# A decoder layer's cross attention: unnormalised exponentials are turned and weighed, and the reciprocal sums, spread over rows by transposes, are applied to the result

## The reference

```python
qh = split_heads(q @ Wq.T + bq); kh = split_heads(k @ Wk.T + bk); vh = split_heads(v @ Wv.T + bv)
scores = einsum('bhqd,bhkd->bhqk', qh, kh) * scale
scores = where(mask == 0, -1e9, scores)
probs = softmax(scores, axis=-1)
out = einsum('bhqk,bhkd->bhqd', probs, vh)
return concat_heads(out) @ Wo.T + bo
```

## Time and profile before

| | |
|---|---|
| median of 3 runs | 1627.44 us (1622.18 to 1630.48) |
| the profiled execution | 1640.67 us |
| its span | 1638.9 us |
| PE busy over the span | 1342.1 us (82%) |
| ACT busy | 893.5 us (55%) |
| DVE busy | 845.1 us (52%) |
| POOL busy | 805.4 us (49%) |
| cross attention | about 764 to 1084 us of the span |

### The profile page before, as it was taken

How to read it: one execution, slowest core, us unless ns; L and a number is a source line. 1 busy time by engine, 2 the same in 40 slices (tenths; PEclk the granted TensorE clock), 3 DMA queues, 4 the chain that set the end, 5 groups by cost and what they waited for, 6 DMA issues and landing times. The chain is left out here.

```text
span 1638.9 us, 31788 instructions
## 1 busy us (share of the span) xinstructions
PE 1342.1 (82%) x10439; PEld 1127.5 (69%) x10439; DVE 845.1 (52%) x1783; ACT 893.5 (55%) x2002; POOL 805.4 (49%) x847
## 2 busy tenths in 40 slices
PE   4999999999999999997877877732699999988300
PEld 4788888888878788885655655522588888887300
DVE  3344444544444444452666576649354454456337
ACT  4677676777767677774255555510355455455101
POOL 2344343444434344454466767601556756667464
PEclk9999999999999999998899999965799999999655
DMA  3200000000000000000223223202254544555234
GB/s 122 73 21 17 19 20 15 20 21 21 15 21 20 15 20 21 8 21 27 76 56 92 74 75 92 62 26 98 84 167 143 175 154 143 173 164 149 71 122 128
DMA packets 123548, 116.45 MB, mean 71 GB/s; under 512 B 42242, under 2 KB 104298, under 8 KB 123434
## 3 DMA queue, kind: packets, MB, share of 16 engines
q1 hardware_dynamic: 116618, 96.23, 19.1%
q0 software_dynamic: 6816, 18.62, 4.2%
HBM read 83.93 MB, written 24.07 MB: 66 GB/s over the span
## 5 line engine op out<-in xcount | busy, mean ns | idle before, releaser
L295 POOL TENSOR_SCALAR_AFFINE_SELECT a_decay<-a_decay 128x256 f32<-128x256 f32 x256 | 110.1, 432 | 271.4 <-ACT a_decay L375 271.4
L498 DVE TENSOR_TENSOR a_probs<-a_ps_s,a_decay 128x384 f32<-128x384 f32 x256 | 131.7, 553 | 171.3 <-PE a_ps_o L673 160.2
L304 POOL TENSOR_TENSOR a_key_sum<-a_probs 128x256 f32<-128x256 f32 x128 | 94.5, 738 | 177.6 <-DVE a_probs L498 165.6
L338 ACT ACTIVATE a_qk_exp<-a_ps_qk 128x512 f32<-128x512 f32 x128 | 76.5, 598 | 137.8 <-PE a_ps_qk L579 130.4
L579 PE MATMUL a_ps_qk<-a_xT_hi,a_w_hi 128*128 128x256 f32 x512 | 144.3, 282 | 3.6 <-ACT a_qk_relu L339 3.6
L491 DVE SCALAR_TENSOR_TENSOR a_qk<-a_qk_exp,a_qk_relu 128x512 f32<-128x512 f32 x128 | 91.3, 713 | 103.7 <-ACT a_qk_relu L339 102.0
L579 PE MATMUL a_ps_qk<-a_xT_hi,a_w_lo 128*128 128x256 f32 x512 | 143.2, 280 | 0.0
L579 PE MATMUL a_ps_qk<-a_xT_lo,a_w_hi 128*128 128x256 f32 x512 | 143.1, 279 | 0.0
L654 PE MATMUL a_ps_s<-a_qk 64*128 64x256 f32 (+1 forms) x1024 | 132.2, 340 | 0.5 <-DVE a_probs L498 0.2
L373 ACT ACTIVATE a_decay<-a_ps_c,a_c_now 128x256 f32<-128x256 f32 x256 | 124.1, 485 | 7.9 <-PE a_ps_c L644 7.4
L961 POOL TENSOR_TENSOR b_probs<-b_probs,b_top 128x1232 f32<-128x1232 f32 x32 | 72.6, 2270 | 103.8 <-DVE b_top L1129 103.8
(11 more groups left out here) (283 smaller groups left out, 4135.1 us busy)
## 6 DMA issues: line engine op xcount, KB each, us to landing
e_gu_raw<-in_L_ffn_gate_w SPq DMA_DIRECT2D x23, 512.0 KB, 3.9
e_gu_raw<-in_L_ffn_up_w SPq DMA_DIRECT2D x23, 512.0 KB, 5.2
e_dn_raw<-in_L_ffn_down_w SPq DMA_DIRECT2D x23, 512.0 KB, 6.3
y_sorted<-e_y_out SPq DMA_DIRECT2D x16, 512.0 KB, 2.9
a_x_in<-in_x SPq DMA_DIRECT2D x16, 256.0 KB, 3.0
a_x_res<-in_x SPq DMA_DIRECT2D x16, 256.0 KB, 2.7
x_rows<-a_x SPq DMA_DIRECT2D x16, 256.0 KB, 2.1
b_x_in<-x_rows SPq DMA_DIRECT2D x16, 256.0 KB
```

Of the source, the lines that this page charges most:

```text
L295: pool.affine_select(out=d, in_=d, compare_op=ALU.is_ge, fill=0.0, base=0, pattern=[[0, 2], [1, P]], channel_multiplier=-1)\
L304: pool.tensor_tensor(key_sum[:], probs[:, :, P:N], probs[:, :, N:TRI], ALU.add).then_inc(keys_summed, 1)
L338: act.activation(qk_exp[:], ps_qk[:], ACT.Exp)
L498: vec.tensor_tensor(probs[:, h, :], ps_s[h][:, 0:TRI], decay[h][:], ALU.mult)\
```

## The change

POOL no longer multiplies the exponentials by the reciprocal sums (`weigh` goes). PE turns the exponentials as they are: `turn_probs` waits for `exp_done`. For each head the reciprocal has to meet the result, whose rows are head features and whose columns are queries. So POOL `widen` writes each reciprocal of a block 16 times side by side (`r_heads`, 128 x 256); PE `spread_rden`, which stands between `weigh_values(b-1)` and `score(b+1, 0)`, turns the two blocks with four 128x128 transposes into `ps_m` (`ps_r`); ACT `keep_r` copies this to `r_wide` in the place of `keep_oT`; and DVE `normalise_o`, which stands between `sums(b, 0)` and `keep_scores(b+1, 0)`, multiplies `ps_o` by `r_wide` into `oT`. `project_o` waits for `normalise_o`. `widen` of a sequence also waits until `spread_rden` of the sequence ahead has read `r_heads`.

```diff
-            def weigh(b, par, blk):
+            def widen(b, par, blk):
                 pool.wait_ge(rden_done, unit(b, blk) + 1)
-                p = probs[par][blk][:, :, 0:S2]
-                pool.tensor_tensor(p, p, over_keys(rden[par][blk]), ALU.mult).then_inc(p_normed, 1)
+                if has(b, -1):
+                    pool.wait_ge(r_made, b)
+                pool.sem_inc(pool_turns, 1)
+                pool.tensor_copy(r_heads[blk][:].rearrange("p (h d) -> p h d", d=DK),
+                                 rden[par][blk][:].unsqueeze(2).to_broadcast([P, H, DK])).then_inc(r_widened, 1)
...
-            def keep_oT(b):
-                act.wait_ge(o_made, b + 1)
+            def keep_r(b):
+                act.wait_ge(r_made, b + 1)
                 if has(b, -1):
-                    act.wait_ge(y_made, b)
-                act.copy(oT[:], ps_o[:]).then_inc(oT_kept, 1)
+                    act.wait_ge(oT_kept, b)
+                act.copy(r_wide[:], ps_r).then_inc(r_kept, 1)
...
+            def normalise_o(b):
+                vec.wait_ge(o_made, b + 1)
+                vec.wait_ge(r_kept, b + 1)
+                if has(b, -1):
+                    vec.wait_ge(y_made, b)
+                vec.tensor_tensor(oT[:], ps_o[:], r_wide[:].rearrange("p t n q -> p t (n q)"), ALU.mult).then_inc(oT_kept, 1)
...
                 keep_scores(b, par, 1)
                 sums(b, par, 0)
+                if has(b, -1):
+                    normalise_o(b - 1)
                 if has(b, 1):
                     keep_scores(b + 1, 1 - par, 0)
...
             def turn_probs(b, par, blk):
                 n = unit(b, blk)
-                pe.wait_ge(p_normed, n + 1)
+                pe.wait_ge(exp_done, n + 1)
...
+            def spread_rden(b):
+
+                pe.wait_ge(r_widened, unit(b, NB))
+                if has(b, 2):
+                    pe.wait_ge(q_kept, b + 3)
+                else:
+                    pe.wait_ge(lg_kept, b - 1)
+                for t in range(2):
+                    for blk in range(NB):
+                        mm = pe.transpose(ps_r[:, t, blk, :], r_heads[blk][:, t * P:(t + 1) * P], ident[:])
+                mm.then_inc(r_made, 1)
...
             def turn_x2(b):
                 pe.wait_ge(x2_ready, b + 1)
+                if has(b, 1):
+                    pe.wait_ge(r_kept, b + 2)
...
                     weigh_values(b - 1, 1 - par, turn - 1 + par)
+                    spread_rden(b - 1)
                 if has(b, 1):
                     score(b + 1, 1 - par, turn + par, 0)
```

More of the change, by code:

```diff
@@ L785, in cross_attention @@
         pT = [sb(f"b_pT{n}", [P, CHUNKS, N]) for n in range(2)]
-        oT = sb("b_oT", [P, 2, N])
+        r_heads = [sb(f"b_r_heads{blk}", [P, 2 * P]) for blk in range(NB)]
+        oT, r_wide = sb("b_oT", [P, 2, N]), sb("b_r_wide", [P, 2, NB, P])
+        r_widened, r_kept = sem("b_r_widened"), sem("b_r_kept")
         resid = sb("b_resid", [P, NB, D])
@@ L798, in cross_attention @@
         ps_lg = ps_m[:, 0, 0:NB * E].rearrange("p (n e) -> p n e", n=NB)
+        ps_r = ps_m[:].rearrange("p t (n q) -> p t n q", n=NB)
         loaded, mask_loaded = cross.loaded, cross.mask_loaded
@@ L812, in cross_attention @@
         s_made, s_kept, top_done, shifted = sem("b_s_made"), sem("b_s_kept"), sem("b_top_done"), sem("b_shifted")
-        exp_done, den_done, rden_done, p_normed = sem("b_exp_done"), sem("b_den_done"), sem("b_rden_done"), sem("b_p_normed")
+        exp_done, den_done, rden_done, r_made = sem("b_exp_done"), sem("b_den_done"), sem("b_rden_done"), sem("b_r_made")
         pT_made, pT_kept, o_made, oT_kept = sem("b_pT_made"), sem("b_pT_kept"), sem("b_o_made"), sem("b_oT_kept")
@@ L961, in shift @@
                 pool.tensor_tensor(p, p, over_keys(top[par][blk]), ALU.subtract).then_inc(shifted, 1)
-            def weigh(b, par, blk):
+            def widen(b, par, blk):
                 pool.wait_ge(rden_done, unit(b, blk) + 1)
-                p = probs[par][blk][:, :, 0:S2]
-                pool.tensor_tensor(p, p, over_keys(rden[par][blk]), ALU.mult).then_inc(p_normed, 1)
+                if has(b, -1):
[3 more added lines that the diff above has]
+                                 rden[par][blk][:].unsqueeze(2).to_broadcast([P, H, DK])).then_inc(r_widened, 1)
             def sequence(b, par, turn):
                 if has(b, -1):
-                    weigh(b - 1, 1 - par, 1)
+                    widen(b - 1, 1 - par, 1)
                 if has(b, 1):
@@ L973, in sequence @@
                 shift(b, par, 1)
-                weigh(b, par, 0)
+                widen(b, par, 0)
                 if has(b, -1):
@@ L984, in _ @@
             all_sequences(pool, sequence)
-            weigh(B - 1, (B - 1) % 2, 1)
+            widen(B - 1, (B - 1) % 2, 1)
             add_bias(B - 1)
@@ L1068, in sequence @@
                 if has(b, -1):
-                    keep_oT(b - 1)
+                    keep_r(b - 1)
                 exponentials(b, par, 1)
@@ L1086, in _ @@
             keep_pT(B - 1, (B - 1) % 2, 1)
-            keep_oT(B - 1)
+            keep_r(B - 1)
             normalise(B - 2)
@@ L1179, in _ @@
             all_sequences(vec, sequence)
+            normalise_o(B - 1)
             add_residual(B - 1)
@@ L1354, in _ @@
             weigh_values(B - 1, (B - 1) % 2, (B - 1) // 2)
+            spread_rden(B - 1)
             project_o(B - 1)
```

## The result

The changed kernel takes 1644.4 us (median of 4 runs, 1643.57 to 1646.28) against 1627.64 of the kernel before (4 runs too): ratio 1.0104, 95% interval 1.0077 to 1.0131. It is 17 us slower; forecast were 14, with a range that holds it.

The account below looks back on a forecast made before the run. Cross attention's period was taken as closed by DVE's path, with no engine full. 14.0 + 0.5 + 1.0 - 1.5 = +14.0 us on the median of 1627.44 gave 1641.4 us; forecast's range 1636 to 1646, whole range 1632 to 1651.

Parts of the forecast that it names:

- What closes the period: Cross attention: DVE's path from the scores to the logits closes each period, 0.2 us behind PE's before, 0.6 after.
- Rival A: Cross attention: the product is hidden and PE's path decides, 0.53 us a period, +7.4 in all, 1634.9 us; chance 0.12.
- `normalise_o` in series: Ahead of `keep_scores`: transposes, copy and product follow one another, so it starts 0.9 to 1.0 us later.
- The price of a period: Cross attention's period grows by 1.0 us, charged in 14 sequences: 14.0 us.
- POOL costs and gives nothing: POOL in cross attention: `weigh` goes, `widen` comes, hidden in the wait for the maxima; gain in a steady period 0.
- The start: Start of cross attention: PE no longer waits for `weigh`, ACT can copy earlier; 1.5 us back, bounds 0 and 2.14.
- The end: End of cross attention: 0.5 us for sequence 15's transposes and 1.0 for the later last residual.
- rival C: Cross attention: TensorE's clock falls more often, 4 to 14 us, some 8 on top, 1649 us; chance 0.14.
- the forecast's mechanism: Cross attention: the added work stands in series ahead of `keep_scores`, 1.0 us a period; +14.0 us in all, chance 0.60.
- The sign that I had named for rival C: Cross attention in the changed profile: a granted clock under 0.85 would show rival C.
- The rule that was cited against the change: TensorE: matmul bursts parted by waits let the clock halve, so the next burst starts slow; no size of its own.

Follow-up runs that it names:

- 8: The changed kernel with DVE's copy of the logits moved ahead of the statistics, nothing else: 1630.72 us, ratio 1.0003 to the kernel before.
- 2: The changed kernel without DVE's product; ACT copies the weighed values after the transposes, output left unnormalised: 1641.21 us, ratio 1.0079 to the kernel before.
- 3: The kernel of experiment 1 with ACT's copy replaced by DVE's product with a tile of ones: 1621.54 us, ratio 0.9949 to the kernel before.
- 5: The changed kernel with the reciprocals' transposes moved into PE's pause in `turn_probs` and their copy moved to DVE: 1623.51 us, ratio 0.9969 to the kernel before.
- experiment 1: The kernel before with only `weigh` removed and nothing added, output left unnormalised: 1624.57 us, ratio 0.9979.
- 4: The changed kernel with `weigh` kept on POOL and the added transposes, copy and product working on ones: 1649.30 us, ratio 1.0121 to the kernel before.
- The filler: The changed kernel with 12 unread identity transposes in PE's pause ahead of `turn_probs`' third group: 1633.10 us, ratio 1.0033 to the kernel before.
- 10: The kernel before with the same 12 idle transposes in its pause ahead of the third group: 1624.16 us, ratio 0.9989.
- e7_early_logits: The kernel of 5 with DVE's copy of the logits moved ahead of the statistics: 1629.57 us, ratio 0.9987 to the kernel before.

## Why the prediction was right, point by point

**What closes the period.** Right. PE waits 0.56 us for the logits at 902.94 (forecast near 0.6, 0.24 before). Moving the logits ahead takes this wait away and shortens the undisturbed period by 0.67 (8). Rival A falls with that, and by 2, which without the product has an undisturbed period 0.33 shorter than the changed kernel's 17.80.

**`normalise_o` in series.** Right. From 894.35 to `keep_scores` 1.97 us; forecast "some 2.0 us". The product is 0.69 instead of 0.65, the handover to it 0.09. It is its place and not its length: 3 and 5 have the same product and their undisturbed periods are those of the kernel before.

**The price of a period.** 0.92 between undisturbed periods, forecast 0.9 to 1.0, taken 1.0. Over the 13 measured periods that is 12.0 us.

**POOL costs and gives nothing.** Right for the steady state: in experiment 1 the undisturbed period is unchanged, and in 4, with POOL's old work back, it is the changed kernel's. `widen` took 0.40 us, below the 0.6 taken and the lower bound of 0.43. The pause in `turn_probs` became one of 2.71 us (forecast 2.5), all for ACT. POOL's busy time in the stage fell by 58 us and not by "about 50": two `weigh` less two copies of 0.40 in each of 16 sequences are 60.

**The start.** Its 1.5 us aren't shown. The first copy of the reciprocals comes 1.0 us earlier than the copy that it replaces, and 1.2 earlier counted from the stage's first scores (819.98 - 800.84 = 19.1 us against 820.97 - 800.62 = 20.4), although the transposes stand ahead of it. But experiment 1, which has the same gain and no transposes, took 819.26 - 797.67 = 21.6 us. The scatter of the start is as large as the term.

**The end.** The term that didn't show: 0.5 for sequence 15 and 1.0 for the last residual. The residual does come 1.1 us later behind the last weighed values (3.51 us behind ACT's last copy against 1075.37 - 1072.35 = 3.02, and that copy 0.6 later), but from the fourteenth copy to the end the stage took 0.2 less. In that part the mean granted clock was 0.81 in the kernel before and 0.92 in the changed one, so the kernel before paid more there to the low clock, and this can hide the 1.5.

**The clock, rival C.** The part of the sum that was missing: I gave it no term. The mean period was forecast at 18.1 us and is 243.0 / 13 = 18.7. Of the 20.7 us of the 13 periods 12.0 are the work in series and 8.7 are low clock beyond what the kernel before already paid. The filler agrees from the other side: it takes 11.3 us off the median, 8.2 off the end of the stage (1102.99 to 1094.84), 10.5 off twelve periods (224.8 to 214.3). So the forecast's mechanism and rival C both happened. The sign that I had named for rival C, a granted clock under 0.85 in the stage, was a bad one: the stage's mean is 0.92, and it was 0.91 before. What showed it was the duration of the query projections.

**How near the sum came.** That the forecast's 14 came near 17 owes much to chance. With the filler in both kernels, so that no projection is slow in either, the change costs 1633.10 - 1624.16 = 8.9 us by the medians, 7 by the ratios (1.0033 against 0.9989), and 9.1 by the end of the profiled stage (1094.84 against 1085.74). So the work in series with the start and the end is worth 7 to 9 us, and not 14; about 8 to 10 are the clock's, to which the sum gave nothing. The series part is less than 14 x 0.92 because the forecast set an undisturbed period beside an undisturbed period, while the mean periods with the filler are 17.9 (214.3 / 12) and 17.1 (205.4 / 12): the kernel before has more of its `turn_x1` at the low clock (10). Two errors of opposite sign met.

The rule that was cited against the change (the Trainium skill, TensorE: Matmul & The Clock Gate, HAM oscillation) holds in direction: filling the pause removes every low projection. The example there has waits on transfers that are longer than the bursts of matmuls between them, while here PE is busy for 186 of 243 us. That a pause by itself decides it is not what the traces show: 1 has the same long pause in its later periods with few low stretches, and 4, with the pause parted in two, has no fewer of them than the changed kernel (481 ns against 458).

Open: what makes a given period fall. The changed kernel's periods alternate, about every second projection slow; e7_early_logits, with the shortest undisturbed period, is hit hardest (512 ns). That it is a matter of how the pauses line up from period to period was not tested.

## What to carry to other kernels

Moving a normalisation behind a product is only cheap if its factor is ready when the product is: cost not the added instructions but the chain from the last operand to the next consumer, and put what doesn't depend on the late operand (here the transposes and the copy) into a wait that already exists. In a chain where PE waits often, measure whether part of a loss is TensorE's clock, by giving PE idle work in its longest pause, in the kernel before as well as in the changed one: the pair separates the clock from the dependency, and an order that is shorter on paper (e7) may lose its gain to the clock until the pause is filled.

## What the runs showed of the hardware that was not expected

- Twelve idle transposes a sequence (about 1.5 us at the high clock) in a pause of 2.7 us kept all later query projections at the high clock (mean 379 ns a matmul against 458 without them and 396 in the kernel before), and gave 11 us of 1644.
- Low stretches hit different instructions at very different prices: in the changed kernel a period with `turn_x1` at the low clock took 18.3 us, one with the query projection there 19.4, against 17.88 for one without either.
- A POOL copy of 16 columns widened to 128x256 took 0.40 us. Of the instructions of the same size in linear attention the affine select (L295) took 0.43 and the addition of two tiles (L304) 0.74.
